# Key features of the encoder kept from the first pass, and layer 1's cross attention without its preparation program

## The reference, cut to what matters

```python
def _softmax_kernel_feats(data, proj, is_query):
    data_dash = jnp.einsum('bnhd,md->bnhm', data * dn, proj)
    diag = jnp.sum(jnp.square(data), axis=-1, keepdims=True) * (dn * dn) / 2.0
    mx = jnp.max(data_dash, axis=-1, keepdims=True) if is_query else jnp.max(data_dash)
    return ratio * (jnp.exp(data_dash - diag - mx) + EPS_KERN)
...
qf = _softmax_kernel_feats(q, proj, True)
kf = _softmax_kernel_feats(k, proj, False)
kv = jnp.einsum('bnhm,bnhd->bhmd', kf, v)
```

## Time and profile before

| | us |
|---|---|
| timed runs | 2778.01, 2778.41, 2785.14 (median 2778.41) |
| profiled execution, its own time | 2784.49 |
| span in its trace | 2782.7 |
| mean granted clock of TensorE | 0.949 |

### The profile page before, as it was taken

One profiled execution on the slowest core, in us unless ns is written; L12 is line 12 of the kernel. 1 busy time (PEld: TensorE's weight loads), 2 busy tenths in 40 slices (PEclk: granted clock), 3 DMA queues, 4 the chain that ended last, 5 costly groups with the idle time before them and its releaser, 6 DMA issues. The chain is left out here.

```text
span 2782.7 us, 94896 instructions
## 1 busy us (share of the span) xinstructions
PE 2604.0 (94%) x39151; PEld 2214.1 (80%) x39151; DVE 1640.8 (59%) x3266; ACT 1478.0 (53%) x4035; POOL 1026.6 (37%) x1208
## 2 busy tenths in 40 slices
PE   6999999999999999998599987999999898899998
PEld 5888888888778888886488985777777677899997
DVE  3555555555575666665555544777777555555553
ACT  3454545555535666665544435777777433444443
POOL 2333333443330000004344444666666323344443
PEclk9999999999999999998699997999999767799999
DMA  6322222222000000000100002011000100000001
GB/s 208 112 85 85 96 97 85 85 91 86 30 1 1 0 0 0 0 0 1 52 1 0 0 0 73 23 28 28 23 28 23 50 0 1 1 0 0 0 0 31
DMA packets 32692, 99.28 MB, mean 36 GB/s; under 512 B 4309, under 2 KB 18265, under 8 KB 27737
## 3 DMA queue, kind: packets, MB, share of 16 engines
q1 hardware_dynamic: 32602, 98.01, 10.6%
HBM read 93.80 MB, written 4.19 MB: 35 GB/s over the span
## 5 line engine op out<-in xcount | busy, mean ns | idle before, releaser
L566 POOL TENSOR_TENSOR l_probs<-l_probs,l_rden 128x1024 f32<-128x1024 f32 x128 | 242.2, 1893 | 429.1 <-DVE l_rden L424 429.1
L508 ACT ACTIVATE l_probs<-ps,l_nmax 128x257 f32<-128x257 f32 x512 | 236.0, 474 | 226.4 <-DVE l_nmax L418 226.4
L973 POOL TENSOR_TENSOR l_probs<-l_probs,l_rden 128x1024 f32<-128x1024 f32 x128 | 242.3, 1893 | 172.3 <-DVE l_rden L843 172.3
L418 DVE TENSOR_REDUCE l_nmax<-ps 128x2 f32<-128x514 f32 x256 | 165.5, 688 | 217.3 <-PE ps L303 217.3
L913 ACT ACTIVATE l_probs<-ps,l_nmax 128x257 f32<-128x257 f32 x512 | 235.9, 474 | 57.9 <-DVE l_nmax L837 57.7
L2717 POOL TENSOR_TENSOR m_hh<-m_hh,m_comb_t 128x512 f32<-128x512 f32 (+2 forms) x160 | 143.2, 895 | 224.0 <-DVE m_hh L2643 224.0
L303 PE MATMUL ps<-l_ctxQ,l_q 32*128 32x257 f32 x3072 | 202.6, 392 | 7.1 <-ACT l_probs L508 6.4
L837 DVE TENSOR_REDUCE l_nmax<-ps 128x2 f32<-128x514 f32 x256 | 165.4, 688 | 66.0 <-PE ps L743 62.1
L2643 DVE TENSOR_TENSOR m_hh<-ps,m_sg 128x512 f32<-128x512 f32 (+2 forms) x160 | 95.6, 598 | 180.2 <-ACT m_sg L2485 180.0
L848 DVE COPY l_pT<-ps 128x512 f32<-128x512 f32 x256 | 164.9, 686 | 53.9 <-PE ps L752 49.7
L343 PE MATMUL ps<-l_pT,l_ctxK 128*32 128x128 f32 x6144 | 194.3, 275 | 0.8 <-DVE l_pT L461 0.8
(11 more groups left out here) (362 smaller groups left out, 6832.2 us busy)
## 6 DMA issues: line engine op xcount, KB each, us to landing
l_ctxQ<-in_ctx_q SPq DMA_DIRECT2D x32, 1542.0 KB, 6.5
l_ctxT<-in_ctx_t SPq DMA_DIRECT2D x32, 385.5 KB, 3.3
l_ctxK<-in_ctx_k SPq DMA_DIRECT2D x32, 384.0 KB, 3.1
x<-in_x SPq DMA_DIRECT2D x4, 512.0 KB, 7.4
scratch<-l_W SPq DMA_DIRECT2D x2, 1024.0 KB, 4.8
l_last_w<-scratch SPq DMA_DIRECT2D x32, 64.0 KB
out_x<-x SPq DMA_DIRECT2D x1, 2048.0 KB, 8.7
m_w<-in_m_w SPq DMA_DIRECT2D x3, 512.0 KB, 4.7
```

What stands on the lines that cost most here:

```text
L418: nc.vector.tensor_reduce(nmax[:, par, 2 * half:2 * half + 2], ps[:, S_B + 2 * half:S_B + 2 * half + 2, 0:NK], AX.X, ALU.max, negate=True) ...
L508: nc.scalar.activation(probs[:, par, hg, :], ps[:, S_B + hg, 0:NK], ACT.Exp, bias=nmax[:, par, hg:hg + 1], accum_out=den[:, par, hg:hg + 1 ...
L566: nc.gpsimd.tensor_tensor(pr, pr, rden[:, b, :, None].to_broadcast([P, HG, NK - 1]), ALU.mult).then_inc(norm_ok, 1)
L973: nc.gpsimd.tensor_tensor(pr, pr, rden[:, b, :, None].to_broadcast([P, HG, K_W]), ALU.mult).then_inc(norm_ok, 1)
```

## The change

**Encoder.** The first pass now holds one tile of tokens stationary and streams the weights, so that a unit is one tile's key dash, tokens on the partitions. The ACT copies each unit from PSUM into one of six buffers, the DVE takes the maximum from there, and SP stores the buffer (512 KB) to a DRAM array `kept`. The ACT reuses a buffer when its maximum and its store are done. When all stores have landed, SP loads the tiles back one by one into two buffers `dash`, two tiles ahead. The second pass has no `project` of `W_DK`; `exponent_k` reads `dash`. The steps are reordered: Q and its dash are projected two tiles ahead, V moves to the bank pair of the query dash, and `eq` has two buffers. Seven steps are unrolled instead of four. The normalisation of x in the first pass is shared by ACT and DVE.

**Layer 1's cross attention.** The weights and the contexts of tiles 0 and 1 are loaded during `stage_moe0`, with a third context buffer; the row of ones is filled there too, first on POOL. There is one program instead of two: its preparation stands at the head of it, and `W` is made in the first tile by the PE and the DVE. `clear_sems` moves from behind `stage_moe0` to ahead of it.

```diff
-def stage_heads(nc, k, w, ctx_t, ctx_l, last_mask, scratch, next_loads):
+def heads_weights(nc, ctx, w, ctx_t, ctx_l, last_mask):
+    bufs["ctxl"], bufs["last_m"], bufs["ctxT"] = sb("ctxl", [CA, B]), sb("last_m", [P, SEQ]), sb("ctxT", [CA, 3, SEQ * NK])
+    loads += [(bufs["ctxT"][0:C, j, :], ctx_t[t]) for t, j in ((0, 2), (1, 1))]
...
-            @block.tensor
-            def _(pe):
-                pe.wait_ge(w_in, 16 * len(loads))
...
-            load(0, 0)
-            sp.dma_start(last_m[:, :], last_mask).then_inc(m_in, 16)
-            sp.dma_start(scratch, W[:, :, :].rearrange("p h d -> p (h d)")).then_inc(w_out, 16)
-            load(1, 1)
+            load(2, 0)
...
+            sp.wait_ge(w_sb, 4)
+            sp.dma_start(scratch, W[:, :, :].rearrange("p h d -> p (h d)")).then_inc(w_out, 16)
...
+                    if first and b == 0:
+                        for g in (2, 3):
+                            pe.wait_ge(w_sb, g - 1)
+                            last_rows(g)
...
+            nc.tensor.matmul(ps[:, T_B + 1, 0:B], va[:, :], ctxl[:, :], start=True, stop=True).then_inc(made, 1)
+            nc.tensor.matmul(ps[:, O_B, 0:B], ka[:, :], ctxl[:, :], start=True, stop=True).then_inc(made, 1)
+            keys_values(0, 2)
...
             scores(0, 0)
+            pe.wait_ge(v_ok, 2)
+            pe.wait_ge(masked, 1)
+            for g in range(2):
+                last_rows(g)
             pe.wait_ge(kv_sb, 2)
-            keys_values(2, 0)
+            keys_values(2, 2)
...
-def stage_performer(nc, k, bufs):
+def stage_performer(nc, k, bufs, kept):
...
-            BA, BB, BC, BD = 0, 2, 4, 6
+            BA, BB, BD, BC = 0, 2, 4, 6
...
+            held = [qsq, ksq, qfT, kfT, va[:, 0, :], va[:, 1, :]]
...
+                for u in range(T):
+                    sp.wait_ge(ev_ok, u + 1)
+                    sp.dma_start(kept[u], held[u % NH][:, :]).then_inc(stored[u % NH], 16)
+                for n in range(NH):
+                    sp.wait_ge(stored[n], 16 * len(range(n, T, NH)))
+                for t in range(2):
+                    fetch(t, t)
+                with sp.Fori(0, T // 2 - 1) as i:
+                    for j in range(2):
+                        sp.wait_ge(subk_ok, 2 * i + j + 1)
+                        fetch(2 * i + j + 2, j)
...
                 def step(t, j, has, turns):
                     if has(-1):
                         pe.wait_ge(at_ok, t)
                     if has(0):
                         pe.wait_ge(eq_ok, t + 1)
+                        turn(BB, eq[:, j, :], tq_mm)
                         pe.wait_ge(ek_ok, t + 1)
                         if has(-1):
                             pe.wait_ge(res_ok, t)
                         turn(BD, ek, tk_mm)
...
-                        project(BD, W_DK, 1 - j, dk_mm)
-                        pe.wait_ge(ksq_ok, t + 2)
-                        project(BA, W_V, 1 - j, v_mm)
+                        pe.wait_ge(sub_ok, t + 2)
+                        project(BC, W_V, 1 - j, v_mm)
+                    if has(2):
+                        pe.wait_ge(xt_ok, t + 3)
+                        if has(1):
+                            pe.wait_ge(ksq_ok, t + 2)
+                        project(BA, W_Q, j, q_mm)
...
                         values(j)
+                    if has(2):
+                        if has(1):
+                            pe.wait_ge(va_ok, t + 2)
+                        project(BC, W_DQ, j, dq_mm)
...
+                def keep(u):
+                    act.wait_ge(d_mm, u + 1)
+                    if u >= NH:
+                        act.wait_ge(max_ok, u - NH + 1)
+                        act.wait_ge(stored[u % NH], 16 * (u // NH))
+                    nc.scalar.copy(held[u % NH][:, :], both(PAIRS[u % 3])).then_inc(ev_ok, 1)
...
+                act.wait_ge(max_ok, T)
+                for n in range(NH):
+                    act.wait_ge(stored[n], 16 * len(range(n, T, NH)))
                 run(act, step)
...
-                def step(t, j, has):
+                def step(t, j, has, turns):
                     if has(1):
-                        diagonal(dq, qsq, qsq_ok, dq_ok, t + 1)
+                        exponent_q(t + 1, 1 - j)
                     if has(-1):
                         residual(t - 1, 1 - j)
-                    if has(1):
-                        exponent_q(t + 1)
                     if has(0):
                         softened(t)
...
                         diagonal(dk, ksq, ksq_ok, dk_ok, t + 1)
-                        exponent_k(t + 1)
+                        exponent_k(t + 1, 1 - j, turns)
+                    if has(2):
+                        diagonal(dq, qsq, qsq_ok, dq_ok, t + 2)
...
+            nc.gpsimd.memset(next_ones, 1.0).then_inc(row_ok, 1)
```

More of the change, by code:

```diff
@@ L653, in stage_heads @@
+        ka, va, wq, wo, hm4, hm, qb, ctxl, last_m, ctxT = [bufs[n] for n in (
+            "ka", "va", "wq", "wo", "hm4", "head_mask", "qb", "ctxl", "last_m", "ctxT")]
+        qbs = sb("qbs", [P, 1])
+        wom, wohm = sb("wom", [P, HG, D]), sb("wohm", [P, H, D])
+        klast, vlast = sb("klast", [P, B]), sb("vlast", [P, B])
+        W = sb("W", [B, H, D])
+        made, v_ok, masked, w_sb = sem("made"), sem("v_ok"), sem("masked"), sem("w_sb")
         K_W, V_AT = NK - 1, NK
-        ctxT = sb("ctxT", [CA, 2, SEQ * NK])
@@ L796, in tile @@
                     if b < 1 or not last:
-                        if b == 1:
+                        if b == 1 and not first:
                             pe.wait_ge(ctx_in[1 - j], 16 * fills)
                         pe.wait_ge(kv_sb, u + 3)
-                        keys_values((b + 3) % SEQ, j if b < 1 else 1 - j)
+                        keys_values((b + 3) % SEQ, 2 if first and b < 1 else j if b < 1 else 1 - j)
                     if b == 0 and not last:
@@ L810, in tile, with last_rows @@
                         values(u - 2, (b - 2) % SEQ, j if b >= 2 else 1 - j, o_free=not (first and b == 2))
+            def last_rows(g):
+                nc.tensor.matmul(ps[:, (T_B + 1, O_B)[g % 2], :], vlast[:, :], wohm[:, HG * g:HG * g + HG, :],
+                                 start=True, stop=True).then_inc(made, 1)
+            nc.tensor.matmul(ps[:, T_B + 1, 0:B], va[:, :], ctxl[:, :], start=True, stop=True).then_inc(made, 1)
+            nc.tensor.matmul(ps[:, O_B, 0:B], ka[:, :], ctxl[:, :], start=True, stop=True).then_inc(made, 1)
+            keys_values(0, 2)
+            pe.wait_ge(kv_sb, 1)
+            keys_values(1, 2)
             turn_x(0)
             queries(0)
-            pe.wait_ge(ones_ok, 1)
-            pe.wait_ge(ctx_in[0], 16)
-            keys_values(0, 0)
-            pe.wait_ge(kv_sb, 1)
-            keys_values(1, 0)
             pe.wait_ge(qbd_ok, 1)
@@ L871, in tile @@
                         maxima(u + 1, (b + 1) % SEQ, 1)
+                    if first and b == 0:
+                        kept_rows(2)
+                        kept_rows(3)
                     if b == 3 and not first:
@@ L941, in tile @@
                         normal(t + 2)
+            act.wait_ge(made, 1)
+            nc.scalar.copy(vlast[:, :], ps[:, T_B + 1, 0:B]).then_inc(v_ok, 1)
+            act.wait_ge(made, 2)
+            nc.scalar.copy(klast[:, :], ps[:, O_B, 0:B]).then_inc(v_ok, 1)
+            store_kv(0, 0, 0)
             rstd_act(nc, k, act, ln)
@@ L945, in _ @@
             normal(0)
+            store_kv(1, 1, 0)
             turned(0)
@@ L1067, in stage_performer, with _, fetch @@
             by_par = lambda ap: ap.rearrange("p (r c) n -> p r c n", r=2)
+            @block.sync
+            def _(sp):
+                def fetch(t, j):
+                    sp.dma_start(dash[:, j, :], kept[bass.ds(t, 1), :, :].rearrange("t p n -> p (t n)")
+                                 ).then_inc(back[j], 16)
+                for u in range(T):
[9 more added lines that the diff above has]
+                        fetch(2 * i + j + 2, j)
+                for j in range(2):
+                    sp.wait_ge(back[j], 8 * T)
             def run(eng, step):
@@ L1260, in normal @@
                         act.wait_ge(xt_mm, g - 1)
-                    for n in range(4):
+                    for n in (2, 3):
                         t = 4 * g + n
@@ L2747, in _, with program @@
             sp.wait_ge(stored, 16)
-def program(nc, d, out, scratch):
+def program(nc, d, out, scratch, kept):
     with ExitStack() as ctx:
@@ L2854 @@
     scratch = nc.dram_tensor("scratch", (B, H * D), F32, kind="Internal").ap()
-    program(nc, aps, out, scratch)
+    kept = nc.dram_tensor("kept", (T, P, H * DH0), F32, kind="Internal").ap()
+    program(nc, aps, out, scratch, kept)
     r = run_bass_kernel_spmd(nc, [{f"in_{n}": a for n, a in arrays.items()}], core_ids=[0])
```

270 lines of the change are left out of this document (127 added, 143 removed).

## The result

The changed kernel takes 2743.8 us (four runs, 2741.8 to 2749.0) against 2778.2 in the same session: a ratio of 0.987, 95% interval 0.984 to 0.990, or 28 to 44 us less. The forecast was 2741.2. That the two are 2.6 us apart is in part luck: the term of the encoder was 12 us too high, and a stage that the change doesn't touch scatters by more than the difference.

What follows compares the result with a forecast made beforehand. The PE was taken as the bound, busy 94% of the span. Gains of 23.7 us (encoder) and 13.5 us (layer 1) sum to 37.2, taking the median from 2778.41 to 2741.2 us, range 2722 to 2761.

Steps and rivals of the forecast that it cites:

- the term of the encoder: Encoder: dropping each tile's key dash in the second pass gains 23.7 us, between 10 and 45.
- Loop tile: Encoder's second pass: a tile takes 12.9 us instead of 13.69, the PE waiting some 0.7 us before its key transposes.
- second ring: Second pass: the PE's path from scores through projections, `values` and query dash to `mx` and back takes 12.7 us.
- Thirty tiles: Encoder's second-pass loop: 0.79 us saved per tile, times 30, gives 23.7 us.
- unrolled code and half clock: Rival: two or three more PE stops in unrolled code and layer 1's low end; gain 28 us, 2750, chance 0.14.
- the DVE keeps its 39.90 us: Encoder's first pass: DVE work stays at 39.90 us, and nobody on the PE waits for its maximum.
- The stores: First pass: 32 stores of 512 KB hide behind 47.6 us of matmuls at cost 0; at 290 GB/s, 10 us more.
- The rival with the stores as the bound: First pass: stores at 290 to 320 GB/s take 5 to 10 us longer than the matmuls; 2757, chance 0.15.
- The first `den`: Hand-over between the encoder's passes: first `den` at 829.7 against 829.9 before, cost 0, up to 7 us more.
- Layer 1: Layer 1's cross attention: first scores 18.5 us earlier, `last_rows` costing about 5; gain 13.5 us, between 8 and 17.
- full clock comes earlier: Layer 1's cross attention: the condition for the upper bound of its gain, 17 us.
- ahead of work that waits for x: Start of `stage_moe0`: the row of ones is one POOL instruction there, given no cost.

Runs made afterwards that it cites:

- e5: Changed kernel with the DVE's residual of the tile before put ahead of `exponent_q` of the next: 2724.2 us.
- e7: Changed kernel with four more unrolled steps of the encoder's second pass behind the loop: 2756.6 us.
- e3: Changed kernel with GpSimd's splitting of the three weight matrices moved behind its splitting of the groups of x: 2753.4 us.
- e9: Changed kernel with every store of kept features issued twice, once to an array that nothing reads: 2788.2 us.
- e8: Changed kernel with residual first, weights split last, new buffer hand-over, second normalisation earlier, row of ones in a POOL gap: 2716.9 us, 0.976 of the kernel before.
- e1: Kernel before with only the encoder's part of the change, semaphores cleared ahead of `stage_moe0`: 2756.1 us, ratio 0.9915.
- e2: Changed kernel with the encoder of before, so layer 1's part alone: 2766.2 us, ratio 0.9946 to the kernel before.

## Why the prediction was right or wrong

**Loop tile: right.** 12.9 us forecast, 12.87 measured; 0.7 us of waiting for `residual` forecast, 0.55 measured; `mx` waits no more. With this wait taken away, e5 has 12.14. One slip in the prediction's second ring had no effect: it adds 1.5 us for `values`, where its own rows give 1.74, so that ring is 13.0 and not 12.7, still near the 12.9 taken. That `exponent_k` from SBUF costs the same is right as well: 1.22 us before and after. By the fixed parts that the Trainium skill gives (VectorE: DVE Perf Modes, the section on the TRN2 errata) the gain would have been an estimated 0.065 us each; the trace has 0.00.

**Thirty tiles: the term left out.** From the first `den` to the last are 31 tiles; 0.82 x 31 would be 25.4 us, and the stretch gave 18.9. The steady tiles gained what they should. The other 6.5 us are the two long tiles behind the loop (2.2 and 2.4 more than 12.87) and the 11.80 of the last tile before, 1.9 less than 13.69. At the loop's start both kernels have two long tiles (15.91 and 16.04 before, 15.12 and 15.30 after), so these cost nothing new. The prediction had the stop of the earlier trace rows, put one to three more into the range, and nothing into the sum. That was the condition of its rival "unrolled code and half clock", which named a gain of 28 us, the gain by landmarks. e7 prices it: 1.2 to 1.8 us for each unrolled step (4.9 and 7.2 us for four), so 4 to 5 us for the three more that the change unrolls.

**First pass: wrong, "the DVE keeps its 39.90 us".** I moved "a part" of the normalisations to the DVE and priced only what the ACT lost by it. The two of each group (0.59 us) still would have fitted; beside GpSimd's splitting they take 2.7 to 3.1, and 4 x 1.13 + 2.7 = 7.2 us is more than the group's matmuls. e3 takes 4.3 of the 5.0 us back. The Trainium skill (SBUF — State Buffer, Who interferes with whom) has this rule: DVE and GpSimd share a pair of SBUF ports, a `tensor_scalar` from SBUF to SBUF can run in a mode that needs it, and whoever comes first holds it for the whole instruction, while a `tensor_reduce` never contends. The trace agrees in both: the normalisation beside GpSimd 2.54 us at most for 0.34, the maxima 1.20 to 1.22 in every row. It was the rule that spoke against this part of the change, and the prediction doesn't use it.

**The stores: right that they cost nothing in the pass** (the ACT waits only for the PE, and e9 shows 382 GB/s when they are the bound, inside my 290 to 415). The Trainium skill (DMA: Bandwidth & Descriptors, Specifications) has about 358 GB/s as one core's limit; the 382 over 85 us is above it, and the measurement decides. The rival with the stores as the bound had the right size for the pass, 5 us, and the wrong cause.

**The first `den`: late by 9 us, mostly before the hand-over.** It came at 838.7 instead of 829.7. Against the kernel before (829.9) 0.9 us are the later start of the stage in that execution, 1.6 the PE's start (3.9 us of waiting for the DVE's second normalisation, of which e8 gave back 0.6), 5.0 the pass, 1.3 the way from the last feature to `den`. In e1, where the clock was not at half there, that last stretch is 18.2 us for 20.3, and 19.0 in the kernel before; so at the full clock the hand-over costs nothing, as forecast.

**Layer 1: right mechanism, near the size.** First scores 10.5 us behind the start for 11 forecast. The stretch from the first to the last scores grew by 2.2 us (474.4 for 472.2; again 473.8 for 472.4, 1.4), where 5 were forecast for `last_rows`. The 5 was not far off for `last_rows` itself: from scores to scores, 3.50 us in later tiles, the first four steps take 5.77, 5.03, 3.58 and 3.58, 4.0 us over. What the sum left out is that the old tile 0 was slow as well: 4.11, 4.11, 5.00 and 3.63, 2.9 us over, at a granted clock of 0.50 and then 0.86 (stretches above). After the change the full clock comes back within 10 us of the first scores. That is the "full clock comes earlier" of the prediction's upper bound; no run has one of the two without the other, so this split is read from the starts and not shown by an experiment. On the other side stand two costs that the prediction put at nothing. The rows of `last_w`, "in tile 1", come late: the PE waits for them for 0.55 us in the changed kernel (from 0 to 2.3 us in the others with the new `stage_heads`), and not at all in the two profiles of before and in e1. And the row of ones, "ahead of work that waits for x", costs 1.5 us: it stands beside the DVE's LayerNorm operations, which the whole stage waits for. e8 gives 1.6 back.

**Sum.** Forecast 23.7 + 13.5 = 37.2. By landmarks 11.7 + 16.3 = 28.0, of which 12 to 14 are layer 1's own. The timed runs say 34.4, with 28 to 44 as their interval: the scatter of `stage_alibi` lies in it, and the 2.6 us between forecast and result are no measure of how good the working was. How the 28 and the 34 go together in detail stays open; 28.0 lies at the very edge of the interval (28.3). Of the encoder's 12 us too many, layer 1's part made up 2.8 and the difference between 28.0 and 34.4 another 6.4: that is the luck in the number. Open too is why e1 gained 3.0 us between `stage_moe0` and `stage_alibi`, 1.7 beyond the 1.3 of the moved clearing.

## What to carry to other kernels

When work moves to an engine, price it on the engine that receives it, next to what its neighbour does in the same microseconds: a cover of 39.9 in 49 us was gone with two small instructions. When a step is taken off the bound, walk the rings of what is left before ordering the rest, and place the operation that someone waits for ahead of the one nobody waits for. And compare landmarks over stretches that the change touches: a stage with unchanged code moved by 15 us here, and the start of the encoder by 8.

## What the runs showed of the hardware

- A `tensor_scalar` of 128 columns from SBUF to SBUF took up to 2.54 us beside a GpSimd instruction, 0.34 alone; one of 32 columns 1.81 for 0.17 beside a memset.
- In unrolled code the PE stood still for 1.7 to 2.6 us at a time, 6 to 35 us apart, while the instruction queue carried packets of 16 KB; in the loop the queue carried none in 300 us.
- Stores of 512 KB in rows of 4 KB held 382 GB/s for 85 us.
- A PE wait of 2.3 us for a DMA, in e2, was followed by a granted clock of 0.83 over 10 us, and these tiles took 3.4 us longer than in the changed kernel with its wait of 0.55.
- One and the same stage took 188.8 to 211.8 us in twelve executions, with a mean granted clock of 0.77 in the shortest and 0.63 in the longest; its matmuls have the same shortest and longest times in each.
